# A two-layer pointwise mixing kernel: 64x64 block-diagonal matrix tiles in place of 32x32 ones, and regions of 12 tiles in place of 15

## What is computed

```python
def _L0_conv_ref(x, W1, b1, W2, b2, c, L_multiplier, init_L):
    rel = jnp.tril(idx[:, None] - idx[None, :]).astype(jnp.float32)
    threshold = jnp.abs(L_multiplier * init_L)
    pos = jnp.maximum(rel.max(axis=-1), threshold)[:, None]
    nd = jnp.log(jnp.abs(c * rel) + 1.0) / (jnp.log(jnp.abs(c * pos) + 1.0) + EPS)
    h = jax.nn.relu(nd[..., None] * W1[0] + b1)
    bias = jnp.einsum('qkm,mh->qkh', h, W2) + b2
    return x + bias.transpose(2, 0, 1)[None]

def _L1_conv_ref(inputs, qw1, qw2, kw1, kw2, qdd, kdd, w):
    wi = w + jnp.eye(m, dtype=w.dtype)
    ret = jnp.einsum('BGMTS,GMN->BGNTS', x, wi)
    hq = jnp.einsum('BGMTS,BTGIM->BGITS', x, qw1)
    ret = ret + jnp.einsum('BGITS,BTGIM->BGMTS', hq, qw2)
    hk = jnp.einsum('BGMTS,BSGIM->BGITS', x, kw1)
    ret = ret + jnp.einsum('BGITS,BSGIM->BGMTS', hk, kw2)
    ret = ret + jnp.einsum('BGMTS,BTGM->BGMTS', x, qdd)
    ret = ret + jnp.einsum('BGMTS,BSGM->BGMTS', x, kdd)
```

## Time and profile before

| What | Value |
|---|---|
| Time, median of 3 runs | 907.83 us (904.5 to 908.47) |
| Span of the profiled execution | 930.2 us |
| TensorE busy in it | 741.4 us |
| VectorE, ScalarE, GpSimd busy | 452.3, 387.6, 432.9 us |
| Moved by DMA | 149.63 MB |

### The profile page before, as it was taken

The page is one execution under the profiler, slowest core; times in us unless marked ns, Lnnn a source line. Parts: engine busy times, 40 slices in busy tenths (PEclk is TensorE's granted clock), DMA queues, the critical chain, the costliest instruction groups (busy, mean ns, idle before and its releaser), DMA issues. The chain is left out here.

```text
span 930.2 us, 39085 instructions
## 1 busy us (share of the span) xinstructions
PE 741.4 (80%) x18210; PEld 547.7 (59%) x18210; DVE 452.3 (49%) x483; ACT 387.6 (42%) x412; POOL 432.9 (47%) x267
## 2 busy tenths in 40 slices
PE   0678864798678876898799978999689878897984
PEld 0255654576556655666557745677357645676974
DVE  7496522376345533564346524464336524464352
ACT  3958624553463435543433334344233342341200
POOL 3545421254233432365458745586358753581020
PEclk9888887999999999999999999999899988999997
DMA  6787687658975999587976898488875988589068
GB/s 132 183 172 140 147 180 167 145 100 190 194 180 125 183 184 201 124 183 161 223 156 129 174 181 192 94 172 172 182 162 110 199 178 151 106 176 227 5 155 200
DMA packets 301055, 149.63 MB, mean 161 GB/s; under 512 B 30045, under 2 KB 296669, under 8 KB 300893
## 3 DMA queue, kind: packets, MB, share of 16 engines
q1 hardware_dynamic: 231456, 113.56, 56.9%
q10 hardware_dynamic: 69436, 33.58, 17.0%
HBM read 77.61 MB, written 69.47 MB: 158 GB/s over the span
## 5 line engine op out<-in xcount | busy, mean ns | idle before, releaser
L451 POOL TENSOR_TENSOR hidden<-log_table,row_scale 128x1024 f32<-128x1024 f32 x192 | 365.4, 1917 | 367.4 <-PE bias L757 359.5
L743 PE MATMUL main<-homes,mats_b 32*32 32x120 f32 (+1 forms) x9216 | 286.5, 272 | 119.6 <-issue 83.3
L743 PEld LDWEIGHTS main<-homes,mats_b 32*32 32x32 f32 x9216 | 257.9, 133 | 187.5 <-issue 136.1
L490 ACT ACTIVATE hidden<-hidden,b_col 128x1024 f32<-128x1024 f32 x192 | 220.3, 1149 | 310.3 <-POOL hidden L451 205.1
L732 PEld LDWEIGHTS main<-homes,mats_a 32*32 32x32 f32 x8192 | 238.1, 129 | 78.6 <-issue 54.9
L732 PE MATMUL main<-homes,mats_a 32*32 32x128 f32 x8192 | 258.8, 275 | 23.7 <-issue 23.6
L657 DVE SCALAR_TENSOR_TENSOR homes<-bias,b_col,homes 64x512 f32<-64x512 f32 (+1 forms) x256 | 185.8, 747 | 174.9 <-DMA homes<-in_x 106.5
L757 PE MATMUL bias<-hidden,w_blocks 128*64 128x512 f32 x768 | 207.6, 648 | 17.7 <-DVE b_col L620 8.8
L639 DVE TENSOR_TENSOR homes<-main,homes 128x1024 f32<-128x1024 f32 x128 | 156.8, 1225 | 107.7 <-PE main L732 104.6
L629 DVE COPY homes<-main 128x960 f32<-128x960 f32 x64 | 74.1, 1157 | 179.7 <-PE main L743 179.5
L517 ACT ACTIVATE homes<-main 128x960 f32<-128x960 f32 (+1 forms) x80 | 71.1, 891 | 109.4 <-PE main L743 99.3
(11 more groups left out here) (37 smaller groups left out, 32.2 us busy)
## 6 DMA issues: line engine op xcount, KB each, us to landing
homes<-in_x SPq DMA_DIRECT2D x200, 192.0 KB, 6.5
out_mixed<-homes ACTq DMA_DIRECT2D x104, 192.0 KB, 5.9
out_mixed<-homes SPq DMA_DIRECT2D x104, 192.0 KB, 5.6
homes<-in_x SPq DMA_DIRECT2D x72, 256.0 KB, 7.1
homes<-in_x SPq DMA_DIRECT2D x136, 64.0 KB
mats_in<-a_mats SPq DMA_DIRECT2D x128, 64.0 KB
out_mixed<-homes ACTq DMA_DIRECT2D x28, 256.0 KB, 8.0
out_mixed<-homes SPq DMA_DIRECT2D x28, 256.0 KB, 5.8
```

Source lines behind the costliest of these rows:

```text
L451: nc.gpsimd.tensor_tensor(hidden_tile(u, g).rearrange("p (j s) -> p j s", j=ROWS), bass.AP(logs.tensor, logs.offset, [list(logs.ap[0]), [1 ...
L490: nc.scalar.activation(hidden_tile(u, g), hidden_tile(u, g), ACT.Relu, bias=b1_col[:, 0:1])\
L743: mm = pe.matmul(main[of_group(g), i % 2, j * W:j * W + REGION_TILES[k] * ROWS], b_weights(g, C * ROWS + j), y_column(k, g, C * ROWS + j), ...
```

## The change

GS goes from 2 to 4: a group is 64 partitions with four blocks, its block-diagonal matrices are 64x64, and there are two groups instead of four. Each step so has 16 matmuls in place of 32, each over twice as many rows and columns of the array. The block-diagonal matrices take twice the space (`mats_b` and `mats_a`), which comes off the homes: 13 tiles each, for regions of 12. The first region keeps 8 tiles, and ten of 12 follow. A home has one tile more than a region, so a load of x never reaches into the next home, and its sixth piece and the wait for it go. The loads of x now are five pieces, at other tiles of the loop. Four buffers of the setup move out of the homes into `mats_in` and `mats_a`. The zeroing of `mats_b` covers twice the columns, and `spread_unit` writes 1024 values per partition in place of 512.

```diff
--- before.py
+++ after.py
@@ -10,7 +10,7 @@
 S = 1024
 W = 128
 BLOCKS = S // W
-GS = 2
+GS = 4
 GROUPS = BLOCKS // GS
 GP = H * GS
 HID = 32
@@ -19,16 +19,17 @@
 COLS = ROWS * W
 COL_TILES = W // ROWS
 BANK = 512
-REGION_TILES = (8,) + (15,) * 8
+REGION_TILES = (8,) + (12,) * 10
 REGIONS = len(REGION_TILES)
 FIRST_TILE = [sum(REGION_TILES[:k]) for k in range(REGIONS)]
 ALL_TILES = S // ROWS
 HALF_TILES = ALL_TILES // 2
-HOME_TILES = max(REGION_TILES)
+HOME_TILES = max(REGION_TILES) + 1
 HOMES = 3
-STORE_PIECES = {8: (2, 3, 3), 15: (2, 3, 3, 3, 4)}
-LAST_STORES = (2, 3, 3, 3, 2, 1, 1)
-LOAD_PIECES = {8: (1, 3, 4), 15: (1, 3, 3, 3, 4, 1)}
+STORE_PIECES = {8: (2, 3, 3), 12: (2, 3, 3, 4)}
+LAST_STORES = (2, 3, 3, 2, 1, 1)
+LOAD_PIECES = {8: (1, 3, 4), 12: (1, 3, 3, 3, 2)}
+X_PIECES = 5
 PORTIONS = (2, 2)
 CHUNK = 32
 CHUNK_TILES = CHUNK // ROWS
@@ -92,10 +93,10 @@
         spare_0 = homes[:, (REGION_TILES[0] + 1) * COLS:HOME_TILES * COLS]
         spare_2 = homes[:, (2 * HOME_TILES + REGION_TILES[0]) * COLS:HOMES * HOME_TILES * COLS]
         comp = {"a": spare_2[:, 0:2048], "b": spare_2[:, 2048:4096]}
-        term = {"a": spare_0[:, 0:2048], "b": spare_2[:, 4096:6144]}
+        term = {"a": spare_0[:, 0:2048], "b": mats_a[:, 0:2048]}
         turned = term
-        first = {"a": spare_2[:, 6144:6400], "b": spare_2[:, 6400:6656]}
-        second = {"a": spare_2[:, 6656:6912], "b": spare_2[:, 6912:7168]}
+        first = {"a": mats_in[:, 0:256], "b": mats_in[:, 256:512]}
+        second = {"a": mats_in[:, 512:768], "b": mats_in[:, 768:1024]}
         diag = {"a": spare_0[:, 2048:2176], "b": spare_0[:, 2176:2304]}
         w_eye = spare_0[:, 2304:2560]
         ident = spare_0[:, 2560:2688]
@@ -129,7 +130,7 @@
         const_bias_made = sem("const_bias_made")
         const_bias_read = sem("const_bias_read")
 
-        x_in = [sem(f"x_in{i}") for i in range(6)]
+        x_in = [sem(f"x_in{i}") for i in range(X_PIECES)]
         a_in = [sem(f"a_in{i}") for i in range(A_RING)]
         unit_ready = sem("unit_ready")
         b_in = sem("b_in")
@@ -306,10 +307,7 @@
 
             def load_x(k, i):
                 T, n = piece_start(load_pieces(k), i), load_pieces(k)[i]
-                if k >= 1 and T + 1 >= HOME_TILES:
-
-                    sp.wait_ge(out_done[0], times(store_pieces, 0, k - 1) * PER_PIECE)
-                elif k >= 2 and T + 1 < REGION_TILES[k - 2]:
+                if k >= 2 and T + 1 < REGION_TILES[k - 2]:
                     left = piece_of(store_pieces(k - 2), min(T + n, REGION_TILES[k - 2] - 1))
                     sp.wait_ge(out_done[left], times(store_pieces, left, k - 2) * PER_PIECE)
                 t0 = tile_of(k, T) * ROWS
@@ -370,29 +368,27 @@
             load_x(1, 4)
             sp.wait_ge(tables_made, 3)
             sp.dma_start(late_scales, scale_late).then_inc(scales_out, DMA)
-            loaded = [3, 5] + [0] * (REGIONS - 2)
+            loaded = [3, X_PIECES] + [0] * (REGIONS - 2)
             for k in range(REGIONS):
 
-                while k + 1 < REGIONS and loaded[k + 1] < 5:
+                while k + 1 < REGIONS and loaded[k + 1] < X_PIECES:
                     load_x(k + 1, loaded[k + 1])
                     loaded[k + 1] += 1
-                if k == 2:
+                if k == 3:
                     sp.wait_ge(scales_out, DMA)
                     sp.wait_ge(nd_ready, PART // 2 // ROWS)
                     sp.dma_start(row_scale[:, 0:PART // 2], late_scales[:, 0:PART // 2]).then_inc(scales_in, DMA)
-                if k == 4:
+                if k == 6:
                     sp.wait_ge(nd_ready, PART // ROWS)
                     sp.dma_start(row_scale[:, PART // 2:], late_scales[:, PART // 2:]).then_inc(scales_in, DMA)
                 for T in range(REGION_TILES[k]):
                     v = chunk_behind(tile_of(k, T))
                     if v is not None:
                         load_mats_a(v)
-                    if k + 1 < REGIONS and T == min(6, REGION_TILES[k] - 4):
-                        load_x(k + 1, 5)
                     for i in range(len(store_pieces(k))):
-                        if T == piece_start(store_pieces(k), i + 1) - 1 - (i == 4 and k < REGIONS - 1):
+                        if T == piece_start(store_pieces(k), i + 1) - 1 - (i == 3 and k < REGIONS - 1):
                             store_upper(k, i)
-                    if k + 2 < REGIONS and T in (7, 10, 13):
+                    if k + 2 < REGIONS and T in (6, 9, 11):
                         load_x(k + 2, loaded[k + 2])
                         loaded[k + 2] += 1
             for i in range(len(out_done)):
```

## The result

| What | Before | After |
|---|---|---|
| Time, median | 907.32 us (4 runs, 904.5 to 908.47) | 879.56 us (4 runs, 872.41 to 881.12) |
| Ratio after / before | | 0.9646, 95% interval 0.9566 to 0.9726 |
| Span of the profiled execution | 930.2 us | 878.2 us |

The change makes the kernel 3.5% faster, by 28 us. The prediction was 835 us, a gain of 72, and 790 to 885 as the range. The time lies in the range, and the gain is less than half of the one that was forecast.

What follows compares the result with a forecast made beforehand. TensorE was taken as the bound, its largest waits being stops for instruction blocks. Terms -93 - 12 + 11 - 12 + 11 + 6 + 15 = -74 us gave a span of 856, scaled by 907.83 / 930.2 to 835 us; range 790 to 885.

Steps and rivals of the forecast that it cites:

- Fetch (-93): TensorE's stops for instruction blocks: 82 blocks for 143, stops falling from 108.4 us to near 15, so -93 us.
- Streaming (+11): TensorE's steps: serial part stays, b steps of 96 columns take 1.42 us, 160 of them for 128: +11 us.
- Rival 3: TensorE's a and b steps: loading 64-column weights shows, +112 us over 4,864 records, 945 us, slower; chance 0.08.
- Clock (-12): TensorE's clock falls to its lower level behind long idle times; fewer stops give -12 us, bounds 0 and -30.
- Start (-12): Start of second and third regions: waits for loads of x go or shrink, -12 us, bounds 0 and -19.
- The bias chain (+11): Second half: two shorter b steps no longer cover the 3.16 us until the next bias tile: +11 us.
- GpSimd: GpSimd's units take twice as long, 66 us more, 499 in all; no cost expected, up to +15 us.
- PSUM term: Evictions from PSUM: VectorE's copy behind a ScalarE relu misses a b step of 1.42 us: +6 us, bounds 0 and +15.
- DMA (+15): First half: transfers limit before TensorE does; 56 tiles lose 0.27 us each, +15 us, bounds 0 and +40.
- Rival 1: Whole kernel: DMA holds more of it, a span of 875 us and a time of 854 us; chance 0.17.
- named as right: Profile signs: near 82 packets, issue waits under 30 us, b steps near 1.4, DMA share above 0.8, among others.
- named as wrong: Profile signs: issue waits of 60 us or more, a steps above 2.0, or TensorE waits moved elsewhere, above 40 each.

Runs made afterwards that it cites:

- before_again: The kernel before, unchanged, profiled a second time: span 898.0 us, against 930.2 in its first profile.
- contiguous_b: The changed kernel with the b matrices stored so that a matmul's 64 weights lie side by side in a partition: 843.05 us, ratio 0.9293 to the kernel before.
- regions_only: The changed kernel with GS back at 2, so 32x32 tiles in four groups, keeping regions of 12: 955.18 us, ratio 1.0522 to the kernel before.
- forms: A separate kernel of matmuls alone, varying tile shape, streamed columns and weight spacing: 64x64 with 96 columns, 83 ns a record contiguous, 0.11 us strided.

## Why the prediction was wrong, point by point

**Fetch (-93): right.** The change leaves 83 packets (82 were worked out) and no stop, where 15 us were allowed for. Against the first profile that is -108.4, against before_again -88.6. It does not hang on the b steps being slow: contiguous_b, whose b steps are as fast as forecast, has the same 83 packets and 1.4 us of stops. regions_only shows the other side: 159 packets, 128.7 us.

**Streaming (+11): the step that failed.** "The serial part of a step stays: 8 matmuls after one another in each group" was the assumption, and "96 columns give 1.42 us" what followed of it: the load of the weights was put at nothing. A b step takes 1.85 us, (451.41 - 447.72) / 2. The b steps' busy time rose by 58 us against the first profile and by 344.5 - 277.2 = 67 against before_again (its groups: 257.3 and 19.9), where +11 was forecast. What holds a record back is its load: 64 weights a partition, 512 bytes apart, take 0.11 us, against 96 x 0.84 = 81 ns of streaming. The rows of before could not show it: 32 strided weights take 57 ns, hidden under 120 columns (101 ns) and just level with the 54 ns of 64 columns.

That last point made the slope of 0.011 us a column a little too low, since its lower end, the step with 64 columns, stood at the load already. From 120 to 96 columns in 32x32 tiles two steps fall from 3.51 us to 2.87 (regions_only), which is 0.013 a column. With contiguous weights 64x64 tiles take the same, where the forecast's slope would give 3.51 - 2 x 0.27 = 2.97:

```profile
435.06 2.88 PE L750 MATMUL main<-homes,mats_b 64*64 64x96 f32 x64
```

(timeline of TensorE, contiguous_b). The whole of that kernel takes 843 us, where 835 were forecast for one whose steps go by streaming. The removal of this one cause gives back 36 of the 45 us of the miss; that the rest is only 8 us is in part luck. Against before_again, contiguous_b's other waits of TensorE grow by 54.6 us (37.2 to 91.8), where the terms for start, bias chain, PSUM and DMA add up to +20, and its busy time falls by 29.6 us (733.8 to 704.2), where streaming and clock together make about nothing.

**Rival 3 named the right thing with the wrong price and place.** "Loading 64-column weights shows" had a chance of 0.08 and was to make the kernel slower by 112 us over all 4,864 records. It cost 47 to 56 us beyond the 11 of the sum, in the b steps alone (47.4 by regions_only). In the a steps 128 columns cover it: they are even 10 us shorter. The two arguments against it were true and did not apply. The bias tiles load 64 columns under 512 columns of streaming, from weights that lie side by side, and the steps of 64 columns loaded 32. The transposes, on which the price rested, load contiguous weights.

The rule of the Trainium skill (TensorE: Matmul & The Clock Gate, section LDWEIGHTS), columns / 1.2 ns, gives, as an estimate, 53 ns for 64 columns. The runs come near it for contiguous weights (58 ns from record to record with 32 columns streaming, forms) and not for weights 16 bytes or more apart (0.11 us). That loads overlap only with matmuls of other row groups, as its section on packing small matmuls says, the runs do not bear out: one tile alone, of 128 rows and 64 contiguous weight columns, streams 96 columns in 8.1 / 96 = 84 ns a record, which leaves no room for a load outside the stream.

**Clock (-12): seen against the first profile only.** The granted clock was 0.934 in the first profile, from which the term was taken, 0.948 in before_again and 0.948 after. By span and clock that is about 123, 93 and 91 us at the lower of the two levels (an estimate). TensorE's busy time between the two profiles of the kernel before differs by 7.6 us. The timed runs lie at 0.931 to 0.95 before and at 0.948 to 0.959 after, so a part of the term can have come; no run parts it from the rest. The stops that went left others of 4 to 9 us in the b steps, behind which the clock falls as well.

**Start (-12): the first half right.** The second region's b steps begin at 112.14 us, where they began behind the wait of the earlier trace rows; VectorE has no wait for x there. The loads for the third region still cost TensorE 3.7 and 6.1 us there.

**What becomes tight.** The bias chain (+11) costs nothing from 48 us on: with b steps of 1.85 us it is covered. With b steps of 1.4, in contiguous_b, it comes as worked out, 13.6 us in 23 waits from 48 us on. GpSimd: nothing, as said (488.2 us busy for 499). Of the PSUM term no wait tells by itself.

**DMA (+15): right in kind.** TensorE's waits for ScalarE and VectorE in the b steps rose from 28.7 us (16.4 + 7.8 + 4.5) in before_again to 48.3; behind the longest of them VectorE and ScalarE wait for x. Rival 1, whose price was 19 us above the forecast, is a part of what is left once the loads are fast: contiguous_b has 68.4 us of them.

**The end of the kernel: no term, and 6 us.** The last a steps run faster without stops, but the last stores do not. TensorE's last records before (before_again) and after:

```profile
887.40 3.74 PE L732 MATMUL main<-homes,mats_a 32*32 32x128 f32 x72 [2.57 <-issue]
843.49 22.06 PE L728 MATMUL main<-homes,mats_a 64*64 64x128 f32 x384
```

From their end to the end of the span it is 6.9 us before (898.0 - 891.1) and 12.6 after (878.2 - 865.6).

**The sum, against before_again.** Stops -88.6; waits for other engines 37.2 to 51.4, so +14.2; TensorE's busy time 733.8 to 782.6, so +48.8; the end +5.7. That makes -19.9, for 19.8 measured between the spans.

**The signs.** Of those named as right, the packets (83), the "issue" waits (none), the a steps (from two to three of them 5.74 - 3.91 = 1.83 us), GpSimd (488.2 us) and the second region's start came; b steps near 1.4 did not, nor did a DMA share above 0.8 (0.77 from 150 to 830 us). Of those named as wrong, waits behind loads of x above 40 us came, or nearly (48.3 with all of its kind). Slow weights were looked for in the a steps, where 128 columns hide them.

## What to carry to other kernels

Ask of every small matmul which of three things takes longest: streaming its columns, loading its weights, or bringing its instructions. Larger tiles halve the instructions, but they double the columns to load, and a load can only hide behind streaming that lasts as long; when one side of a step shrinks (120 to 96 columns) and the other grows (32 to 64), price both. Look at the spacing of the weights in memory before anything else: an access pattern that costs nothing with one tile shape can set the pace with the next.

## What the runs showed of the hardware that was not expected

- A load of fp32 weights runs at two rates. With 4 or 8 bytes between the weights of a partition a serial record with 64 columns of weights takes 58 to 60 ns; with 16, 32, 64 or 512 bytes, 110 to 120 ns. It is in the length of the loads too: the b steps' LDWEIGHTS average 203 ns in the changed kernel and 138 in contiguous_b, with the same matmuls.

```profile
L739 PEld LDWEIGHTS main<-homes,mats_b 64*64 64x64 f32 x5632 | 329.9, 203 | 114.5 <-issue 50.2 <-ACT homes L513 48.0 <-DVE homes L625 13.2
```

```profile
L750 PEld LDWEIGHTS main<-homes,mats_b 64*64 64x64 f32 x5632 | 247.7, 138 | 144.7 <-ACT homes L515 69.2 <-issue 52.1 <-DVE homes L632 21.3
```

(groups by form: the changed kernel, then contiguous_b.)
- The loads of different tiles of the array do not add up: two tiles of 64x64 take what one takes (both 10.9 us for 96 serial records, weights 512 bytes apart).
- Stops for instructions do not fall in proportion to the packets. 143 packets cost 88.6 and 108.4 us, 159 cost 128.7, and 83 none, or 1.4 us with the faster b steps of contiguous_b.
